# Stage two of a mixture-of-experts kernel: next rows' transposes, their copy and their quantisation at other places in the order

## The chip, the cores and the metric

The kernel runs on one core of a Trainium2 chip. The metric is device time in microseconds. Before the change three runs took 254.97, 255.40 and 255.97 us, median 255.4.

## What is computed

2048 rows of 512 numbers go through two expert layers. The first picks one of four experts by token id and uses one matrix three times, in f32 split into two halves. The second picks one of eight experts by the largest router logit, with weights cut to -1, 0, 1 and rows quantised to 8 bits ahead of each product:

```python
x = x + xattn(_layernorm(x), token_ids, ctx, ctx, ctx)      # silu(h W.T) * (h W.T), then W
x = x + ffn(_layernorm(x), router_w, wg, wu, wd)

def _weight_quant(w):
    s = 1.0 / jnp.clip(jnp.mean(jnp.abs(w)), EPS, None)
    return jnp.clip(jnp.round(w * s), -1.0, 1.0) / s
def _act_quant(x):
    s = 127.0 / jnp.clip(jnp.max(jnp.abs(x), axis=-1, keepdims=True), EPS, None)
    return jnp.clip(jnp.round(x * s), -128.0, 127.0) / s
# ffn, for every expert e, kept where the argmax of the logits is e
g = bitlinear(xf, wg[e])
u = bitlinear(xf, wu[e])
y = bitlinear(jnp.square(jax.nn.relu(g)) * u, wd[e])
```

## The kernel before, in words

Rows are sorted by expert into slots of 128, so that a slot has one expert. Stage one has 19 slots, stage two 23 (B2, numbered 0 to 22), which begin at about 172 us of the span. The weights of stage two are reduced to their signs during stage one and stay in SBUF as bf16. EARLY is 5: slots 0 to 4 are laid out before all rows are counted, slots 5 to 22 (late_rows) after.

One slot b of stage two takes this way, and a buffer name ending in 0 or 1 is that of the slot's parity:

- VectorE `quantise(b)` (L1304) makes the int8 rows t8 from the slot's rows, once they have landed (x1_in) and the transposes of slot b-2 have read the same buffer.
- TensorE `transpose_q(b)` (L1687, source t) turns them, in two transposes of pairs of int8, into PSUM bank 0. ScalarE `evict_tT(b)` (L783) copies that to qT.
- TensorE `gate_product(b)` and `up_product(b)` (L1695, source qT), each four matmuls 128x128 by 128x512. `load_ffn_expert` (L1707) loads the number of the next slot's expert into a register of TensorE's queue, by which the products pick their weights.
- ScalarE `relu_of(b)` (L791) and `square_of(b)` (L799); VectorE `product_of(b)` (L1314, prod), `largest_product` (L1324), `inverse_largest` (L1336) and `scale_from` (L1347); ScalarE `quantise_prod(b)` (L834) makes r8.
- TensorE `transpose_r(b)` (L1687, source r), ScalarE `evict_rT(b)` (L807), TensorE `down_product(b)` (L1695, source rT). VectorE `output(b)` (L1368) scales and adds; GpSimd computes the scale of the output (L642) and scatters the rows to memory (L652).

Each engine has its order written out by hand, in the five blocks of the program, and runs it strictly; semaphores join them. The slots overlap: at step u TensorE works on the gate and up products of slot u, the transposes of rows u+1, and transposes and down product of slots u-2 and u-3. ScalarE and VectorE have their own lists of steps u. SyncE loads the rows of each slot from memory (L411), in the order of the slots.

Of the kernel before, what the change touches and what calls it, by code (L numbers as in the profile page):

```python
# [24 lines left out]
B2 = TILES + E2 - 1  # L25
# [25 lines left out]
EARLY, EARLY_AFTER = 5, 14  # L51
# [42 lines left out]
def moe_program(nc, x_in, tokens_in, ctx_in, router_in, weights_in, out):  # L94
    with ExitStack() as whole:
# [161 lines left out]
        def cols_of(slots, col, n=1):  # L257

            if slots[0] < EARLY:
                tile, first = staged[slots[0] // 3], slots[0] % 3  # L260
            else:
                tile, first = late_rows, slots[0] - EARLY
            if len(slots) == 1:
                return tile[:, first * ROW + col:first * ROW + col + n]
            three = tile[:, first * ROW:(first + len(slots)) * ROW].rearrange("p (s c) -> p s c", c=ROW)
            return three[:, :, col:col + n]
# [16 lines left out]
        def pairs(transposed):  # L283
            return transposed.bitcast(I8)
# [397 lines left out]
        def _(act):  # L682
# [92 lines left out]
            def evict_tT(b):  # L775
                if not 0 <= b < B2:
                    return
                act.wait_ge(tT_ready, b + 1)
                if b >= 2:
                    act.wait_ge(u_ready, b - 1)  # L780
                else:
                    act.wait_ge(a_ready, B1)
                nc.scalar.activation(qT[b % 2][:, :], pairs(tT_ps), ACT.Copy).then_inc(qT_ready, 1)  # L783

            def relu_of(b):
                if not 0 <= b < B2:
                    return
                act.wait_ge(g_ready, b + 1)
                if b >= 1:
                    act.wait_ge(relu2_ready, b)  # L790
                nc.scalar.activation(relu[:, :], g_ps[b % 2][:, :], ACT.Relu).then_inc(relu_ready, 1)  # L791

            def square_of(b):
                if not 0 <= b < B2:
                    return
                act.wait_ge(relu_ready, b + 1)
                if b >= 1:
                    act.wait_ge(prod_ready, b)
                nc.scalar.activation(relu2[:, :], relu[:, :], ACT.Square).then_inc(relu2_ready, 1)  # L799

            def evict_rT(b):
                if not 0 <= b < B2:
                    return
                act.wait_ge(rT_ps_ready, b + 1)
                if b >= 2:
                    act.wait_ge(d_ready, b - 1)
                nc.scalar.activation(rT[b % 2][:, :], pairs(rT_ps), ACT.Copy).then_inc(rT_ready, 1)  # L807
# [16 lines left out]
            def copy_by_slot(late):  # L824
                act.wait_ge(blocks_ready, late + 1)
                nc.scalar.activation(by_slot[late][:, :], by_slot_ps[late], ACT.Copy).then_inc(by_slot_ready, 1)

            def quantise_prod(b):
                if not 0 <= b < B2:
                    return  # L830
                act.wait_ge(r_scale_ready, b + 1)
                if b >= 1:
                    act.wait_ge(rT_ps_ready, b)
                nc.scalar.activation(r8[:, :], prod[b % 2][:, :], ACT.Copy, scale=fac[b % 2][:, 2:3])\  # L834
                    .then_inc(r8_ready, 1)
# [47 lines left out]
            evict_tT(3)  # L883
            for u in range(2, B2 - 1):
                relu_of(u)
                if u in (3, 4, B2 - 2):


                    evict_tT(u + 1)
                square_of(u)  # L890
                if 4 < u < B2 - 2:
                    evict_tT(u + 1)
                if u == 4:
                    copy_by_slot(1)
                evict_rT(u - 2)
                quantise_prod(u - 1)
# [11 lines left out]
        def _(dve):  # L908
# [387 lines left out]
            def quantise(b):  # L1296
                if not 0 <= b < B2:
                    return
                dve.wait_ge(x1_in[b], 16)
                if b >= 2:  # L1300
                    dve.wait_ge(tT_ready, b - 1)
                else:
                    dve.wait_ge(hT_ready, B1)
                dve.tensor_scalar(t8[b % 2][:, :], cols_of([b], 0, D), cols_of([b], NEG), cols_of([b], SCALE),  # L1304
                                  ALU.add, ALU.mult).then_inc(t8_ready, 1)
# [207 lines left out]
            product_of(3)  # L1513
            for u in range(4, STEPS):
                largest_product(u - 1)
                if u > 4:
                    quantise(u + 1)
                if u in (B2 - 2, B2):
                    output(u - 4)
                inverse_largest(u - 1)  # L1520
                if u not in (B2 - 2, B2):
                    output(u - 4)
                scale_from(u - 1)
                product_of(u)

        @block.tensor
        def _(pe):
# [191 lines left out]
            def transpose_q(b):  # L1719
                if not 0 <= b < B2:  # L1720
                    return
                pe.wait_ge(t8_ready, b + 1)
                if b >= 1:
                    pe.wait_ge(qT_ready, b)
                    if b == EARLY + 1:

                        pe.wait_ge(by_slot_ready, 2)
                else:

                    pe.wait_ge(hT_lo_ready, B1)  # L1730
                transpose2(tT_ps, t8[b % 2]).then_inc(tT_ready, 1)

            def gate_product(b):
                if not 0 <= b < B2:
                    return
                pe.wait_ge(qT_ready, b + 1)
                if b >= 2:
                    pe.wait_ge(relu_ready, b - 1)
                if b == 0:

                    pe.wait_ge(cut_ready, MATS - 1)
                    pe.wait_ge(p_ready, B1)
                if b == 1:
                    pe.wait_ge(by_slot_ready, 1)
                product2(g_ps[b % 2], qT[b % 2], ffn_expert[b], 0).then_inc(g_ready, 1)

            def up_product(b):
                if not 0 <= b < B2:
                    return
                if b >= 2:  # L1750
                    pe.wait_ge(prod_ready, b - 1)
                if b == 0:
                    pe.wait_ge(pT_lo_ready, B1)
                if b == 1:
                    pe.wait_ge(x1T_copied, B1)
                product2(u_ps[b % 2], qT[b % 2], ffn_expert[b], 1).then_inc(u_ready, 1)
# [101 lines left out]
            transpose_r(0)  # L1858
            for u in range(3, B2 - 2):
                gate_product(u)  # L1860
                up_product(u)
                load_ffn_expert(u + 1)
                if u == 4:
                    spread_means(1)
                transpose_q(u + 1)
                transpose_r(u - 2)
                down_product(u - 3)

# [50 lines left out]
```

## Time and profile before

| what | value |
|---|---|
| median of three runs | 255.4 us |
| the profiled execution | 255.78 us |
| its span | 253.8 us |
| TensorE busy | 233.1 us, 92% |
| VectorE busy | 216.7 us, 85% |
| ScalarE busy | 210.9 us, 83% |
| GpSimd busy | 165.8 us, 65% |
| chain of waits, share of TensorE | 69% |
| granted TensorE clock | 0.996 |

The span goes from the first to the last instruction of the program; the execution takes about 2 us more. The busy time of TensorE (PE) is that of its matmuls, whose records overlap in a pipeline; PEld is its weight load. DVE is VectorE, ACT ScalarE, POOL GpSimd, SP SyncE. A small q behind an engine (PEldq, SPq) is its queue, the part that reads instructions and issues them. An engine that is not on the chain of waits may idle without cost. Times in the trace are microseconds from the start of the span.

### The profile page before, as it was taken

Reading aid. Unit: us, or ns where it says so; the run is one execution under the profiler, and the core shown is the slowest. Engines: PE = TensorE matmul, PEld = TensorE weight load, DVE = VectorE, ACT = ScalarE, POOL = GpSimd, SP = SyncE. Lnnn points to the kernel's source line nnn. Section 1 sums busy time; section 2 is a strip of 40 time slices with the busy share of each in tenths; the row PEclk is TensorE's granted clock in tenths of the full one; section 3 lists DMA queues with packets and bytes.
Section 4 is the critical chain, followed back from the end, with each engine's and each line's share of the span. In section 5 each row is a group of like instructions: output and inputs, shape, how many; then the busy total and the mean of one; then the engine's idle time right before and its main releaser. Section 6 shows DMA issues by size and latency. Waiting matters only on the chain.

```text
span 253.8 us, 5548 instructions
## 1 busy us (share of the span) xinstructions
PE 233.1 (92%) x1327; PEld 167.8 (66%) x1327; DVE 216.7 (85%) x675; ACT 210.9 (83%) x324; POOL 165.8 (65%) x325
## 2 busy tenths in 40 slices
PE   2398989999999999999999999999999999999980
PEld 2245778888888888888888888885344444444430
DVE  5889989799989988898888988879999888889871
ACT  2776899799888988898888888787898999999960
POOL 4363665868778777687777664347638786757653
PEclk9999999999999999999999999999999999999998
DMA  6999944946664499784576434651389952211110
GB/s 201 423 336 383 425 183 155 355 132 234 240 208 151 131 368 404 284 310 145 210 249 225 161 103 180 207 159 56 98 226 296 313 214 83 85 38 68 65 42 0
DMA packets 13725, 51.70 MB, mean 204 GB/s; under 512 B 2750, under 2 KB 2750, under 8 KB 10112
## 3 DMA queue, kind: packets, MB, share of 16 engines
q1 hardware_dynamic: 8816, 37.91, 42.8%
q0 software_dynamic: 4880, 13.44, 14.4%
q8 instruction: 13, 0.21, 0.4%
q14 instruction: 16, 0.13, 0.1%
HBM read 40.49 MB, written 13.48 MB: 213 GB/s over the span
## 4 chain that ended last, share of the span: by engine, by line
PE 69%; DVE 11%; DMA 11%; issue 5%; POOL 1%; ACT 1%; SPq 0%; DVEq 0%; ACTq 0%; POOLq 0%
PE bank L1573 33%; PE bank L1695 18%; PE bank L1557 8%; PE bank L1665 5%; DMA staged<-weight_chunks 5%; DMA ternary<-weight_chunks 3%; PE bank L1687 2%; DMA x<-x_rows,gather 2%; DVE ctx_lo L1009 1%; POOL out_rows L652 1%; DMA staged<-x_rows 1%; DVE ternary L966 1%; DVE t L1304 1%; DVE stats L1067 1%; PE bank L1592 1%
## 5 line engine op out<-in xcount | busy, mean ns | idle before, releaser
L1695 PE MATMUL bank<-ternary,qT 128*128 x184 | 44.2, 380 | 0.2
L703 ACT ACTIVATE ternary<-staged 128x2048 bf16<-128x2048 f32 x20 | 38.0, 1899 | 2.2 <-DMA staged<-weight_chunks 2.2
L709 ACT ACTIVATE ternary<-staged,w_scale 128x1536 int16<-128x1536 f32 x20 | 31.4, 1576 | 2.3 <-DVE w_scale L1023 0.6
L1695 PEld LDWEIGHTS bank<-ternary,qT 128*128 128x128 bf16 x184 | 17.8, 98 | 21.2 <-issue 6.2
L571 POOL DMA_INDIRECT x_rows<-row,store_at x19 | 25.3, 1330 | 6.8 <-POOL store_at L563 5.3
L482 POOL DMA_INDIRECT x<-x_rows,gather x16 | 18.5, 1155 | 10.4 <-DVE gather L978 6.3
L652 POOL DMA_INDIRECT out_rows<-late_rows,late_token x18 | 19.1, 1059 | 8.7 <-DVE late_rows L1368 6.4
L1695 PE MATMUL bank<-ternary,rT 128*128 x92 | 23.6, 380 | 0.3 <-ACT rT L821 0.3
L756 ACT ACTIVATE p<-bank,rstd 128x512 f32<-128x512 f32 x19 | 13.0, 685 | 12.0 <-PE bank L1573 12.0
L1573 PE MATMUL bank<-ctx_hi,pT_hi 128*128 x76 | 22.3, 415 | 0.1
L1103 DVE SCALAR_TENSOR_TENSOR p<-bank,rstd,p 128x512 f32<-128x512 f32 x19 | 14.2, 750 | 9.6 <-ACT p L756 9.6
L1573 PE MATMUL bank<-ctx_hi,hT_hi 128*128 x76 | 22.3, 414 | 0.0
L1665 PEld LDWEIGHTS bank<-router,x1T 128*128 128x128 f32 x152 | 19.7, 191 | 2.0 <-ACT x1T L765 0.6
L1573 PE MATMUL bank<-ctx_lo,hT_hi 128*128 x76 | 20.4, 390 | 0.2 <-DVE ctx_lo L1009 0.2
L1573 PE MATMUL bank<-ctx_lo,pT_hi 128*128 x76 | 20.6, 392 | 0.0
L1573 PE MATMUL bank<-ctx_hi,pT_lo 128*128 x76 | 20.5, 392 | 0.0
L526 POOL TENSOR_TENSOR row<-ln,half_powers 128x2 f32<-128x2 f32 x19 | 14.5, 763 | 9.1 <-DVE squares L1138 9.1
L1314 DVE TENSOR_TENSOR prod<-bank,relu 128x512 f32<-128x512 f32 x23 | 15.8, 689 | 5.4 <-issue 3.4
L1573 PE MATMUL bank<-ctx_hi,hT_lo 128*128 x76 | 20.3, 389 | 0.0
L1665 PE MATMUL bank<-router,x1T 128*128 128x8 f32 x152 | 18.2, 246 | 0.1
L498 POOL TENSOR_TENSOR rstd<-var_eps,half_powers 128x1 f32<-128x1 f32 x19 | 14.0, 734 | 4.8 <-DVE var_eps L1079 4.3
L834 ACT ACTIVATE r<-prod,fac 128x512 int8<-128x512 f32 x22 | 15.9, 721 | 0.9 <-DVE fac L1347 0.9
(237 smaller groups left out, 646.5 us busy)
## 6 DMA issues: line engine op xcount, KB each, us to landing
staged<-weight_chunks SPq DMA_DIRECT2D x20, 1024.0 KB, 5.3
late_rows<-x_rows SPq DMA_DIRECT2D x18, 260.0 KB, 3.2
ternary<-ctx_chunks SPq DMA_DIRECT2D x4, 1024.0 KB, 6.4
ternary<-weight_chunks SPq DMA_DIRECT2D x4, 1024.0 KB, 12.3
x_rows<-filler SPq DMA_DIRECT2D x1, 2080.0 KB
staged<-x_rows SPq DMA_DIRECT2D x5, 260.0 KB, 2.7
x_rows<-row,store_at POOLq DMA_INDIRECT x19, 6.0
out_rows<-late_rows,late_token POOLq DMA_INDIRECT x18
```

The lines of the kernel that those rows point to most:

```text
L482: pool.indirect_dma_start(x[b % RING], None, x_in, bass.IndirectOffsetOnAxis(ap=gather1[:, b:b + 1], axis=0), bounds_check=last_token, oob ...
L526: pool.tensor_tensor(r[:, RSTD:INV + 1], s[:, 2:4], half_powers[:, :], ALU.pow).then_inc(norm2, 1)
L571: pool.indirect_dma_start(x1_rows, bass.IndirectOffsetOnAxis(ap=store_at[b % ROWS][:, :], axis=0), row[b % ROWS][:, :], None, bounds_check ...
L652: pool.indirect_dma_start(out, bass.IndirectOffsetOnAxis(ap=token, axis=0), cols_of([b], 0, D), None, bounds_check=last_token, oob_is_err= ...
L703: nc.scalar.activation(ternary[:, m * K * D:(m + 1) * K * D], staged_of(i), ACT.Abs, accum_out=abs_sum[:, 2 * i:2 * i + 1]).then_inc(abs_r ...
L709: nc.scalar.activation(ternary[:, m * K * D + DVE_COLS:(m + 1) * K * D].bitcast(I16), staged_of(i)[:, DVE_COLS:], ACT.Copy, scale=w_scale[ ...
L834: nc.scalar.activation(r8[:, :], prod[b % 2][:, :], ACT.Copy, scale=fac[b % 2][:, 2:3])\
L1314: dve.tensor_tensor(prod[b % 2][:, :], u_ps[b % 2][:, :], relu2[:, :], ALU.mult)\
L1557: last = pe.transpose(ps[:, k * P:(k + 1) * P], src[:, k * P:(k + 1) * P], ident[:, :])
L1573: last = pe.matmul(ps[:, :], left[:, k * P:(k + 1) * P], right[:, bass.ds(e * (K * D) + k * D, D)], start=(n == 0 and k == 0), stop=(n == ...
L1665: last = pe.matmul(logits_ps[:, 0:E2], x1T[:, k * P:(k + 1) * P], router[:, k * E2:(k + 1) * E2], start=(k == 0), stop=(k == K - 1))
L1695: last = pe.matmul(ps[:, :], side(left[:, :], k), ternary[:, bass.ds(e * (3 * K * D) + (kind * K + k) * D, D)], start=(k == 0), stop=(k == ...
```

## The change

Three places of the hand-written order move, all of them in stage two, and no instruction is added or removed:

- On TensorE the transposes of the next rows stand between the gate and the up product, at steps 3 and 5 to 20. At step 4 they stay behind the up product.
- On ScalarE the copy of these transposes stands between relu and square at steps 3 to 21. Before it did so at steps 3, 4 and 21 only.
- On VectorE the rows are quantised two slots ahead, from step 4 on. Before it was one slot ahead.

```diff
@@ ScalarE
             for u in range(2, B2 - 1):
                 relu_of(u)
-                if u in (3, 4, B2 - 2):
+                if u > 2:
                     evict_tT(u + 1)
                 square_of(u)
-                if 4 < u < B2 - 2:
-                    evict_tT(u + 1)
                 if u == 4:
                     copy_by_slot(1)
                 evict_rT(u - 2)
@@ VectorE
             for u in range(4, STEPS):
                 largest_product(u - 1)
-                if u > 4:
-                    quantise(u + 1)
+                quantise(u + 2)
                 if u in (B2 - 2, B2):
                     output(u - 4)
@@ TensorE
             for u in range(3, B2 - 2):
                 gate_product(u)
+                if u != EARLY - 1:
+                    transpose_q(u + 1)
                 up_product(u)
                 load_ffn_expert(u + 1)
-                if u == 4:
+                if u == EARLY - 1:
                     spread_means(1)
-                transpose_q(u + 1)
+                    transpose_q(u + 1)
                 transpose_r(u - 2)
                 down_product(u - 3)
```

TensorE, a late step of an even slot, before. Bank 4 takes the gate product, bank 1 the up product, bank 0 the transposes of t8, bank 7 those of r8; ISA is a register instruction of the queue:

```order
L1695 MATMUL bank4<-ternary,qT0 128x512
L1695 ISA
L1695 MATMUL bank1<-ternary,qT0 128x512
...
L1695 MATMUL bank1<-ternary,qT0 128x512
L1707 TENSOR_LOAD expert2_1
L1707 ISA x2
L1687 MATMUL bank0<-ident16,t8_1 128x128 x2
L1687 MATMUL bank7<-ident16,r8 128x128 x2
```

And the same step after:

```order
L1690 MATMUL bank4<-ternary,qT0 128x512
L1682 MATMUL bank0<-ident16,t8_1 128x128 x2
L1690 ISA
L1690 MATMUL bank1<-ternary,qT0 128x512
...
L1690 MATMUL bank1<-ternary,qT0 128x512
L1702 TENSOR_LOAD expert2_1
L1702 ISA x2
L1682 MATMUL bank7<-ident16,r8 128x128 x2
L1690 ISA
L1690 MATMUL bank6<-ternary,rT1 128x512
```

The transposes of t8 have moved ahead of the up product; load and transposes of r8 stay behind it.

ScalarE, one step before (relu2 is the square, qT1 the copy of the next rows' transposes):

```order
L791 ACTIVATE relu<-bank4 128x512
L799 ACTIVATE relu2<-relu 128x512
L783 ACTIVATE qT1<-bank0 128x512
L807 ACTIVATE rT0<-bank7 128x512
L834 ACTIVATE r8<-prod1,fac1 128x512
```

and after:

```order
L791 ACTIVATE relu<-bank4 128x512
L783 ACTIVATE qT1<-bank0 128x512
L799 ACTIVATE relu2<-relu 128x512
L807 ACTIVATE rT0<-bank7 128x512
L834 ACTIVATE r8<-prod1,fac1 128x512
```

The copy has changed places with the square.

VectorE, from one product to the next, before (fac0 holds the largest product of the even slot and its scales):

```order
L1314 TENSOR_TENSOR prod0<-bank1,relu2 128x512
L1324 TENSOR_REDUCE fac0<-prod0 128x1
L1304 TENSOR_SCALAR t8_0<-late_rows 128x512
L1336 RECIPROCAL fac0<-fac0 128x1
L1368 SCALAR_TENSOR_TENSOR late_rows<-bank6,out_scale,late_rows 128x512
L1347 TENSOR_SCALAR fac0<-fac0,cap_scale 128x1
```

and after:

```order
L1310 TENSOR_TENSOR prod0<-bank1,relu2 128x512
L1320 TENSOR_REDUCE fac0<-prod0 128x1
L1300 TENSOR_SCALAR t8_1<-late_rows 128x512
L1332 RECIPROCAL fac0<-fac0 128x1
L1364 SCALAR_TENSOR_TENSOR late_rows<-bank6,out_scale,late_rows 128x512
L1343 TENSOR_SCALAR fac0<-fac0,cap_scale 128x1
```

The place in the row is the same; the buffer is the other one, since the slot is one further on.

## Rows read from the trace of the kernel before

**Rows 1.** Busy time by windows; columns: stretch, length, PE, PEld, DVE, ACT, POOL, clock, DMA

```profile
200.00:220.00 20.00, 19.85 (x105) 9.23 (x103) 17.62 (x39) 18.52 (x34) 15.08 (x30) 1.00 0.45 157
```

**Rows 2.** Page, groups of instructions; busy, mean ns, idle before

```profile
L1695 PE MATMUL bank<-ternary,qT 128*128 x184 | 44.2, 380 | 0.2
```

**Rows 3.** Timeline of one steady step; start, length, engine, instruction, idle before

```profile
197.10 0.69 DVE L1314 TENSOR_TENSOR prod<-bank,relu 128x512 f32<-128x512 f32 x1 [0.24 <-issue]
...
197.63 1.90 PE L1695 MATMUL bank<-ternary,qT 128*128 x8
...
198.43 0.54 DVE L1304 TENSOR_SCALAR t<-late_rows 128x512 int8<-128x512 f32 x1
...
198.70 0.60 ACT L791 ACTIVATE relu<-bank 128x512 f32<-128x512 f32 x1
...
199.33 0.63 ACT L799 ACTIVATE relu<-relu 128x512 f32<-128x512 f32 x1
...
199.37 0.28 PE L1687 MATMUL bank<-ident,t 128*128 128x128 bf16 x2
...
199.48 0.28 PE L1687 MATMUL bank<-ident,r 128*128 128x128 bf16 x2
...
199.60 0.21 DVE L1347 TENSOR_SCALAR fac<-fac,cap_scale 128x1 f32<-128x1 f32 x1
...
199.64 1.03 PE L1695 MATMUL bank<-ternary,rT 128*128 x4
...
199.87 0.58 ACT L783 ACTIVATE qT<-bank 128x512 bf16<-128x512 int8 x1
...
200.05 0.69 DVE L1314 TENSOR_TENSOR prod<-bank,relu 128x512 f32<-128x512 f32 x1 [0.24 <-issue]
...
200.59 1.90 PE L1695 MATMUL bank<-ternary,qT 128*128 x8
```

**Rows 4.** Instructions of line 1707; min/median/max ns, first and last start

```profile
L1707 PEldq TENSOR_LOAD <-expert x23: 301/308/632, 171.4 to 237.4; - x23
```

**Rows 5.** Timeline of PE: first, longest and last step from slot 6 to 21

```profile
191.73 1.89 PE L1695 MATMUL bank<-ternary,qT 128*128 x8
...
206.64 1.90 PE L1695 MATMUL bank<-ternary,qT 128*128 x8
...
208.65 0.27 PE L1687 MATMUL bank<-ident,t 128*128 128x128 bf16 x2
...
209.88 1.89 PE L1695 MATMUL bank<-ternary,qT 128*128 x8
...
237.03 1.03 PE L1695 MATMUL bank<-ternary,qT 128*128 x4
```

**Rows 6.** Timeline of PE, step 3: the transposes of slot 4

```profile
183.57 0.28 PE L1687 MATMUL bank<-ident,t 128*128 128x128 bf16 x2 [0.21 <-DVE t L1304]
```

**Rows 7.** Timeline of SP's queue and of DVE; page, DMA issues

```profile
182.90 5.79 SPq L411 DMA_DIRECT2D late_rows<-x_rows  x6
...
187.02 0.69 DVE L1324 TENSOR_REDUCE fac<-prod 128x1 f32<-128x512 f32 x1
...
late_rows<-x_rows SPq DMA_DIRECT2D x18, 260.0 KB, 3.2
```

**Rows 8.** Timeline of the tail, step 21 and on

```profile
238.10 0.60 ACT L791 ACTIVATE relu<-bank 128x512 f32<-128x512 f32 x1
...
238.74 0.60 ACT L783 ACTIVATE qT<-bank 128x512 bf16<-128x512 int8 x1
...
239.23 0.62 ACT L799 ACTIVATE relu<-relu 128x512 f32<-128x512 f32 x1
...
239.94 0.69 DVE L1314 TENSOR_TENSOR prod<-bank,relu 128x512 f32<-128x512 f32 x1 [0.53 <-ACT relu L799]
...
240.23 0.72 ACT L834 ACTIVATE r<-prod,fac 128x512 int8<-128x512 f32 x1
...
240.84 0.60 ACT L791 ACTIVATE relu<-bank 128x512 f32<-128x512 f32 x1
```

## The prediction, made before the changed kernel ran

> **What bounds the kernel now.** I read the page first: TensorE is busy all along, so the busy share decides nothing, and the change touches only stage two, the last 80 us. The table by windows then shows what stage two looks like [rows 1]: in 20 us TensorE is busy 19.85, but ScalarE 18.52 and VectorE 17.62, so three engines are nearly full and a shorter step of one needs room on the other two. The timeline of one step gives the rest.
>
> The price of a product comes from the page [rows 2]: a matmul record lasts 0.380 us, and eight in a row last 1.90 [rows 3], so they start (1.90 - 0.38) / 7 = 0.217 us apart. A step has twelve, 2.60. The two transposes of t8 begin 0.11 ahead of the two of r8 (199.37, 199.48), so four cost 0.22. TensorE's work in a step is 2.82 us. The step shown lasts 200.59 - 197.63 = 2.96. Its gap is at the gate product: the down product begins at 199.64 and is through its four starts at 200.51, while the copy into qT begins at 199.87, ends at 200.45, and the gate product starts 0.14 behind it, at 200.59. The copy can't come sooner: its transposes ran at 199.37, behind the up product. So each step goes round transposes, copy, gate product, with only one down product to cover the copy.
>
> Over the whole stretch, gate product 6 starts at 191.73 and gate product 21 at 237.03 [rows 5]: 45.30 us for 15 steps, 3.02 each, 0.20 above TensorE's work. The rest over 2.96 is in five longer steps of 3.08 to 3.24 (the longest, 206.64 to 209.88, is shown). There the t8 transposes start 208.65 - 206.64 = 2.01 after the gate product where 8 x 0.217 = 1.74 would do, 0.27 late. What stands between is the load of the next expert's number: 0.31 us as a median and 0.63 at most [rows 4]. TensorE's queue can issue nothing behind it meanwhile.
>
> **The change, part by part.**
>
> *Transposes between gate and up product (steps 3 and 5 to 20).* Same instructions. The copy now has up product, r8 transposes and down product to hide behind, 0.87 + 0.11 + 0.87 = 1.85 us, where it had 0.98. Taken from the gate product's start G: transposes at G + 0.87. The copy is behind relu on ScalarE; relu starts at G + 1.07 (198.70 - 197.63 [rows 3]); the copy follows 0.49 later, G + 1.56, ends at G + 2.15, and the next gate product may go at G + 2.29. TensorE needs until G + 2.82. The wait goes, with 0.5 to spare.
>
> *What is late next on TensorE* is the load of the expert's number. It stays behind the up product, in front of the r8 transposes. As the gate product no longer holds the queue, the queue comes to it earlier, so a short load is covered; the long ones (five of fifteen) cost between 0 and 0.27 each. I take 0.02 a step, near the lower end, because a product behind a held queue (206.64) shows the lateness and I remove the hold. Step: 2.84. The bounds for the step: 2.82, all covered, and 2.96, only the long ones gain nothing more than the row of a short step today.
>
> The Trainium skill, "TensorE: Matmul & The Clock Gate", Engine queue depths, gives TensorE a queue of 64 instructions. By it the loads would be wholly hidden and a step 2.82, the lower bound above. This trace can't confirm the depth, as the gate product is waited for in the steps shown; the sum does without it.
>
> *The copy between relu and square.* ScalarE in this order can be read in the tail, where before has it already [rows 8]: copy to square 0.49, square to r8 1.00 (with the rT copy in it), r8 to relu 0.61. With 0.49 from relu to copy (where the copy needn't wait) that is 2.59 a step, below 2.84. The square starts at relu + 0.98 instead of + 0.63, so the product on VectorE comes 0.35 later: before, square 199.33, ends 199.96, product 200.05, i.e. relu + 1.35; after, relu + 1.70 or G + 2.77. VectorE between two products, without the wait: from the product at 197.10 to the end of the scale at 199.81, 2.71 us [rows 3], again below 2.84, so it keeps up though it runs later against TensorE. Its next link: the scale of product u-1 ends 2.71 after that product, at G - 2.84 + 2.77 + 2.71 = G + 2.64; r8 is wanted at relu + 1.98 = G + 3.05. That leaves 0.4. The round that joins the two engines, r8, relu, copy, square, product (0.61 + 0.49 + 0.49 + 0.72) and on through maximum and scale to the r8 after next (2.71 + 0.1), is 5.12 us for two steps, 2.56 a step. All three engines fit into 2.84.
>
> *Rows quantised two slots ahead.* With the transposes in front of the up product, t8 is wanted 0.87 sooner. Left one slot ahead it would be too late: it starts 1.33 after the product of the step before (198.43 - 197.10 [rows 3]), at G - 2.84 + 2.77 + 1.33 = G + 1.26, ends at G + 1.80, and its transposes are due at G + 0.87. Two ahead, it is done 1.9 before it is wanted. The count of instructions is the same except that t8 of row 6 comes at step 4 instead of 5. Its row must have landed: issues start at 182.90, six in 5.79 us, so row 6 is issued by 184.0 and lands 3.2 later, 187.2 [rows 7]; VectorE reaches it 0.6 after the maximum at 187.02, at 187.6. Hidden, by 0.4. If not, VectorE stands some tenths once.
>
> *Steps 3 to 5.* Here the change costs. The transposes of step 3 wait for t8 of row 4 until 183.57 in both kernels [rows 6]; before, both products of step 3 were ahead of that wait and lay in it, so that TensorE idled only 0.21 by the row. After, the up product is behind it: 183.57 + 0.14 + 0.87 = 184.58. And the load, issued from a queue that was just held, is bare. From the long step: eight issues and a load of 0.63 took 2.01 [rows 4, 5]. Four issues fewer save at most half of the 1.38 beside the load, which leaves 1.32, or 1.00 with a load of 0.31, and there is 0.87 of work to cover it: 0.13 to 0.45 bare, taken as 0.3. Then r8 transposes and down product, 0.98 and the start of a held product 0.14: gate product 4 at 186.0. Step 4 keeps its order, 2.96: 188.96. Step 5 at 2.82: its wait for t8 of row 6 is gone. Gate product 6: 191.78, against 191.73. The loss and the gain of the first steps cancel, 0 +- 0.5.
>
> *Steps 6 to 20*: 15 x (3.02 - 2.84) = 2.7 us saved.
>
> *Tail.* Product 21 starts at 239.94, 2.91 behind gate product 21 [rows 5, 8]; relu is on time (238.10), but the copy waits 0.15 for transposes that wait for t8. After, G + 2.77: 0.15 saved. From there VectorE's chain is as before, ending in the scatters.
>
> Sum: -0.05 + 2.7 + 0.15 = 2.8. The profiled execution took 255.78 (span 253.8): 253.0. The median of the runs shown, 255.4, is 0.38 below it: **252.6 us**.
>
> **The rivals.**
>
> *A. Long loads stay bare.* All five long steps keep 0.2 to 0.27, and step 3 is at its bad end: 1.2 us less gain, 253.8. For it: the load is at the same place against the next transposes [rows 5]. Against: the queue is no longer held at each gate product.
>
> *B. The bound is another engine, nothing is gained.* ScalarE is busy 18.52 of 20 us, VectorE 17.62 [rows 1]. If those waits that look like slack are latency that reappears (product waits for square, r8 for scale), a step stays near 3.0 and time is 255.4 less 0 to 1, about 255. Against: both sums of starts are 2.59 and 2.71. The Trainium skill, "Perfetto Trace Analysis", Identifying the Most-Contended Engine, says to judge TensorE by weight-load busy share and not by matmul busy share. Weight loads are 9.23 of 20 us here, so by that rule ScalarE is the engine to relieve and this is the case that follows; the gap in front of the gate product in the steady step speaks against it, but not against a small remainder.
>
> *C. Slower.* The place is ScalarE's queue, in front of the square. The copy is now ahead of the square, so whatever makes the transposes late (a long load, t8, a bare queue) delays square, product, maximum, scale and r8, all in one line. It decides when the copy is held beyond relu + 0.49 by more than the free part of the two-step round, 2 x 3.02 - 5.1 = 0.9 us, in most steps. If it takes a step to 3.12, 15 x 0.10 = 1.5, with the 1.0 of step 3 not won back at step 5: 255.4 + 2.5 = 257.9. Against: the transposes stand at G + 0.87, 0.4 before their copy's turn, and t8 has a whole step.
>
> **How the numbers follow.** Forecast (252.0 to 253.3) 0.60; A 0.16; B 0.15; C 0.09. A measurement here can tell 0.5% from no change, that is 254.1 to 256.7. Forecast and A are faster, B nearly all same, C slower: 0.76, 0.15, 0.09. The range starts at 251.8 (step 2.82, loads of step 3 covered: 0.3 + 0.3 + a little) and goes to 254.6, the bound of a 2.96 step, which takes in A and the near part of B.
>
> **What would show it.** Gate products 6 to 21 in the trace after: 2.82 to 2.86 apart, the transposes right behind the fourth matmul. No idle between down and gate product. Product behind relu by 1.70. Gate product 4 near 186.0, an idle time at step 3 ahead of the transposes of about 1 us; gate product 6 near 191.8. Wrong if steps stay at 2.95 or more, if r8 waits for its scale, if t8 of row 6 waits for its row, or if waits of 0.2 and more stand in front of the r8 transposes.

## The result, and the profile after

| | before | after |
| --- | --- | --- |
| median of the runs, us | 255.87 (254.97 to 256.35, 6 runs) | 253.19 (252.79 to 253.79, 6 runs) |
| ratio, 95% interval | | 0.990 [0.9878, 0.9922] |
| profiled execution: time, span, us | 255.78, 253.8 | 253.38, 251.4 |
| mean granted clock | 0.996 | 0.994 |

The kernel is faster by 2.7 us, or 1.0%. The forecast was 252.6 in a range of 251.8 to 254.6, from a median of 255.4 for the kernel before; with six runs that median is 255.87, so that 0.47 of the 0.59 between 252.6 and 253.19 lies in the starting point. In the changed kernel the line of the products is 1690, of the transposes 1682, of the load of the expert's number 1702, of the product on VectorE 1310, of its maximum 1320, of t8 1300 and of the scale 1343; ScalarE's lines are the same.

The first answer to read is the table by windows, over the same 20 us as [rows 1], with the same columns:

```profile
200.00:220.00 20.00, 19.89 (x115) 10.10 (x116) 19.06 (x45) 19.20 (x36) 15.68 (x31) 1.00 0.48 170
```

All engines do more in the same 20 us: TensorE 115 matmuls for 105, VectorE 19.06 us for 17.62, ScalarE 19.20 for 18.52. TensorE's busy time hardly moved (19.85 to 19.89), since waits of 0.1 to 0.3 us between matmuls don't show in it.

A steady step of the changed kernel, from the timeline, answers to [rows 3]:

```profile
198.30 1.03 PE L1690 MATMUL bank<-ternary,qT 128*128 x4
...
199.17 0.27 PE L1682 MATMUL bank<-ident,t 128*128 128x128 bf16 x2
...
199.28 1.03 PE L1690 MATMUL bank<-ternary,qT 128*128 x4
199.37 0.60 ACT L791 ACTIVATE relu<-bank 128x512 f32<-128x512 f32 x1
...
199.86 0.59 ACT L783 ACTIVATE qT<-bank 128x512 bf16<-128x512 int8 x1
...
200.14 0.27 PE L1682 MATMUL bank<-ident,r 128*128 128x128 bf16 x2
...
200.75 0.21 DVE L1343 TENSOR_SCALAR fac<-fac,cap_scale 128x1 f32<-128x1 f32 x1
...
201.06 0.69 DVE L1310 TENSOR_TENSOR prod<-bank,relu 128x512 f32<-128x512 f32 x1
...
201.14 1.03 PE L1690 MATMUL bank<-ternary,qT 128*128 x4
201.34 0.73 ACT L834 ACTIVATE r<-prod,fac 128x512 int8<-128x512 f32 x1
```

The copy ends at 199.86 + 0.59 = 200.45, and the gate product follows at 201.14, 0.69 later: it no longer waits for the copy. The step is 201.14 - 198.30 = 2.84. The product stands 201.06 - 199.37 = 1.69 behind relu, and r8 begins 0.38 after the scale's end at 200.96.

Over the stretch of [rows 5], with the steps ahead of it, on the timeline of TensorE:

```profile
184.24 0.28 PE L1682 MATMUL bank<-ident,t 128*128 128x128 bf16 x2 [1.08 <-DVE t L1300]
...
186.61 1.89 PE L1690 MATMUL bank<-ternary,qT 128*128 x8
...
189.58 1.03 PE L1690 MATMUL bank<-ternary,qT 128*128 x4
...
191.55 0.13 PEld L1682 LDWEIGHTS bank<-ident,r 128*128 128x128 bf16 x2 [0.46 <-ACT r L834]
191.58 0.27 PE L1682 MATMUL bank<-ident,r 128*128 128x128 bf16 x2
...
192.68 1.03 PE L1690 MATMUL bank<-ternary,qT 128*128 x4
...
234.90 1.03 PE L1690 MATMUL bank<-ternary,qT 128*128 x4
```

From gate product 6 (192.68) to gate product 21 (234.90) it is 42.22 us, 2.815 a step, where it was 45.30 and 3.02. The first rows are the price. The transposes of step 3 wait 1.08 for t8, not 0.21 [rows 6], and gate product 4 starts 2.37 behind them; before it was 1.38, as the experiment that undoes this place shows again below.

The load of the step shown above, in the form of [rows 4] (over all 23 loads the times are 299, 308 and 674 ns):

```profile
L1702 PEldq TENSOR_LOAD <-expert x1: 674/674/674, 198.9 to 198.9; - x1
```

It is the longest one of this execution. It begins 0.6 behind the gate product's start, and the r8 transposes still come at 200.14, right behind the up product: it costs 0.02 at most (the step is 2.84). Before, one of 632 ns made the long step of 3.24. Not every long load is hidden, though: in a second profile of the same changed kernel (the run beside the experiment on step 3, below) one took 897 ns,

```profile
L1702 PEldq TENSOR_LOAD <-expert x1: 897/897/897, 198.3 to 198.3; - x1
```

and there the r8 transposes came 0.10 late (at 199.65, due at 199.55), the down product another 0.11 late, and the step was 200.75 - 197.70 = 3.05.

And the tail, product 21:

```profile
237.65 0.69 DVE L1310 TENSOR_TENSOR prod<-bank,relu 128x512 f32<-128x512 f32 x1 [0.35 <-ACT relu L799]
```

It is 237.65 - 234.90 = 2.75 behind gate product 21, where it was 239.94 - 237.03 = 2.91. Product 22 wins another 0.11 (2.45 behind product 21, it was 2.56).

The account of the two profiled executions, in us: transposes of step 3 to gate product 6, +0.28 (8.44 for 8.16); 15 steps, -3.08; tail, -0.16 - 0.11. That is -3.07. What lies ahead of it, which the change doesn't touch, put the transposes of step 3 at 184.24 and not 183.57, +0.67. Of this 0.55 is there already at relu of slot 0 (176.23 for 175.68), and it is a difference between executions: in the second profile of the changed kernel that relu starts at 175.66. Together -2.40, the difference of the spans. The medians, with more runs, say -2.7.

### The profile page after: what moved, and what is told of

Its sections match the earlier page's. It is cut to its first block, busy times and chain, and to the rows that moved or that the text cites. A ratio compares the mean times of both kernels' runs of the same rounds, so it can differ in the third digit from the quotient of the medians.

```text
span 251.4 us, 5540 instructions
## 1 busy us (share of the span) xinstructions
PE 229.9 (91%) x1319; PEld 167.5 (67%) x1327; DVE 216.9 (86%) x675; ACT 208.8 (83%) x324; POOL 166.2 (66%) x325
## 4 chain that ended last, share of the span: by engine, by line
PE 72%; DVE 10%; DMA 9%; issue 4%; POOL 1%; ACT 1%; SPq 0%; DVEq 0%; ACTq 0%; POOLq 0%
PE bank L1568 34%; PE bank L1690 20%; PE bank L1552 9%; PE bank L1660 5%; DMA staged<-weight_chunks 5%; DMA ternary<-weight_chunks 3%; PE bank L1682 2%; PE bank L1794 2%; POOL out_rows L652 1%; DMA staged<-x_rows 1%; DVE ternary L962 1%; DVE ctx_lo L1005 1%; PE bank L1587 1%; DMA token_ids<-token_ids_in 1%; DVE ternary L1024 1%
## 5 line engine op out<-in xcount | busy, mean ns | idle before, releaser
L1690 PE MATMUL bank<-ternary,qT 128*128 x179 | 45.4, 379 | 0.7 <-ACT relu L791 0.3
L1690 PEld LDWEIGHTS bank<-ternary,qT 128*128 128x128 bf16 x184 | 17.2, 98 | 16.4 <-issue 1.8
```

The costliest lines, as they stand in the source:

```text
L1690: last = pe.matmul(ps[:, :], side(left[:, :], k), ternary[:, bass.ds(e * (3 * K * D) + (kind * K + k) * D, D)], start=(k == 0), stop=(k == ...
```

## The experiments

My theory: the gate product waits for the copy from PSUM, and with the wait gone TensorE's own work (2.82 us a step) is the bound. It left two things open: which of the three edits takes the wait away, and whether loads of the expert's number cost anything because they are long, or because the queue of TensorE comes to them late. Ratios are against runs of the kernel before on the same chip (medians 255.88, 255.79 and 255.82 for the three groups). A difference can be told from 0.5% on, 1.3 us; below that I lean on the traces. Where a time is divided by 15, it runs from relu of slot 6 to relu of slot 21 in that run's profile (45.31 before, 42.22 after). A load is called bare where TensorE has no work to cover it.

### One part at a time

VectorE's edit alone: in the kernel before, only

```diff
-                if u > 4:
-                    quantise(u + 1)
+                quantise(u + 2)
```

> Of the three edits only the one on VectorE: rows quantised two slots ahead. My theory (the steady step is paced by transposes, copy, gate product): steps 6 to 20 stay at 2.95 to 3.02 us, since t8 was in time there; only the wait for t8 of row 6 at step 5 (0.7) and that at step 21 (about 0.4) go. 0.5 to 1.1 us faster than before, about 255.0 where before is 255.9. Rival (t8 is what the steps wait for, as the tags of the weight loads say): steps fall to 2.82, 3 us faster.

Measured: 255.69, ratio 0.999 [0.9970, 1.0009]. No change that can be told from noise. The wait for t8 at step 5 did go, but gate product 6 then waited for its copy:

```profile
191.65 1.90 PE L1694 MATMUL bank<-ternary,qT 128*128 x7 [0.47 <-ACT qT L783]
```

It starts 191.65 - 188.05 = 3.60 behind gate product 5, where it was 191.73 - 187.92 = 3.81. The new t8 at step 4 stands in front of the scale of product 3 on VectorE, so r8 and behind it relu 5, square and copy came later on ScalarE (r8 1.11 behind gate product 5, before 0.82). So 0.2 us of the expected 0.7 is there. Steps 6 to 20 were 45.70 / 15 = 3.05 long; in this run more loads were long, up to 841 ns. The expectation was too high for the first reason, and what VectorE alone gives is within what the loads vary from run to run.

TensorE and VectorE changed, ScalarE as before (copy behind the square):

```diff
-                if u > 2:
+                if u in (3, 4, B2 - 2):
                     evict_tT(u + 1)
                 square_of(u)
+                if 4 < u < B2 - 2:
+                    evict_tT(u + 1)
```

> TensorE and VectorE as changed, ScalarE as before (copy behind the square at steps 5 to 20). My theory: the copy ends at relu + 1.16 + 0.6 = G + 2.83 and the gate product can start 0.14 later, at G + 2.95 to 2.97, so the wait in front of the gate product stays although the transposes are early. Steps 2.95, the long ones of before gone; the loss of 1 us at step 3 stays: 0.3 faster to 0.5 slower than before. Rival (the place of the transposes is what counts): steps 2.82, as fast as the whole change, 2.7 us faster.

Measured: 256.75, ratio 1.0037 [1.0017, 1.0057]. A step on the timeline:

```profile
207.68 1.04 PE L1694 MATMUL bank<-ternary,qT 128*128 x4
...
208.56 0.28 PE L1686 MATMUL bank<-ident,t 128*128 128x128 bf16 x2
...
208.76 0.60 ACT L791 ACTIVATE relu<-bank 128x512 f32<-128x512 f32 x1
...
209.39 0.63 ACT L799 ACTIVATE relu<-relu 128x512 f32<-128x512 f32 x1
...
209.92 0.58 ACT L783 ACTIVATE qT<-bank 128x512 bf16<-128x512 int8 x1
...
210.64 0.60 PE L1694 MATMUL bank<-ternary,qT 128*128 x2
```

The transposes are there at 208.56, and the copy begins only at 209.92, 1.16 behind relu, because the square is in front of it. The gate product follows the copy's end (210.50) by 0.14, and the step is 2.96, to the hundredth what it was before [rows 3]. So the copy's place on ScalarE alone held the gate product: relu 1.08 behind the gate product, copy 1.16 later, 0.58 for it and 0.14 to start. The early transposes without the copy's new place gain nothing and pay the loss of step 3.

ScalarE and VectorE changed, TensorE as before (transposes behind the up product):

```diff
                 gate_product(u)
-                if u != EARLY - 1:
-                    transpose_q(u + 1)
                 up_product(u)
                 load_ffn_expert(u + 1)
-                if u == EARLY - 1:
+                if u == 4:
                     spread_means(1)
-                    transpose_q(u + 1)
+                transpose_q(u + 1)
```

> ScalarE and VectorE as changed, TensorE as before (transposes of t8 behind the up product). My theory: the copy can run 0.31 after transposes at G + 1.74, so at G + 2.05 to 2.64, and the gate product may start at G + 2.78, just ahead of the 2.82 that TensorE needs: steps 2.82 to 2.88, without the loss at step 3. 2.5 to 3.5 us faster than before, at least level with the whole change; the move on TensorE would then be worth nothing by itself. Rival (the move on TensorE is what brings the gain; without it loads of the expert's number push transposes, copy, square and product all later): steps 2.95 or more, under 1 us faster.

Measured: 252.99, ratio 0.9889 [0.9869, 0.9909]: level with the whole change. The same step:

```profile
208.40 1.89 PE L1690 MATMUL bank<-ternary,qT 128*128 x8
...
210.12 0.28 PE L1682 MATMUL bank<-ident,t 128*128 128x128 bf16 x2
...
210.44 0.60 ACT L783 ACTIVATE qT<-bank 128x512 bf16<-128x512 int8 x1 [0.16 <-PE bank L1682]
...
211.22 1.03 PE L1690 MATMUL bank<-ternary,qT 128*128 x4
```

Here the copy waits 0.16 for transposes behind the up product, and yet the step is 211.22 - 208.40 = 2.82: the copy begins 0.32 behind its transposes, not 0.50 as in [rows 3], and that is enough. Over steps 6 to 20 the copy stands 0.71 to 0.99 behind relu, where 0.49 would do, and the steps take 43.06 / 15 = 2.87. The whole change has 2.815, so the move on TensorE brings about 0.8 us over these steps, and loses 1.0 at step 3.

Without VectorE's edit, the other two in place:

```diff
-                quantise(u + 2)
+                if u > 4:
+                    quantise(u + 1)
```

> TensorE and ScalarE as changed, VectorE as before (rows quantised one slot ahead). My theory: a ring closes, transposes, copy (+0.31), square (+0.49), product (+0.72), maximum, t8 (+1.33 and 0.54), transposes (+0.1): 3.47 us a step in place of 3.02. 16 steps: 6 to 8 us slower than before. Rival (t8 has slack enough): as fast as the whole change.

Measured: 266.13, ratio 1.0395 [1.0352, 1.0438], more than expected. A step:

```profile
208.54 0.69 DVE L1310 TENSOR_TENSOR prod<-bank,relu 128x512 f32<-128x512 f32 x1 [0.87 <-PE bank L1691]
...
209.26 1.03 PE L1691 MATMUL bank<-ternary,qT 128*128 x4
...
209.87 0.54 DVE L1300 TENSOR_SCALAR t<-late_rows 128x512 int8<-128x512 f32 x1
...
210.46 0.29 PE L1683 MATMUL bank<-ident,t 128*128 128x128 bf16 x2 [0.17 <-DVE t L1300]
210.58 1.03 PE L1691 MATMUL bank<-ternary,qT 128*128 x4
...
211.29 0.63 ACT L799 ACTIVATE relu<-relu 128x512 f32<-128x512 f32 x1
...
211.85 0.27 PE L1683 MATMUL bank<-ident,r 128*128 128x128 bf16 x2 [0.24 <-issue]
212.01 0.69 DVE L1310 TENSOR_TENSOR prod<-bank,relu 128x512 f32<-128x512 f32 x1 [0.77 <-PE bank L1691]
...
212.95 1.03 PE L1691 MATMUL bank<-ternary,qT 128*128 x4
```

t8 ends at 210.41 and its transposes go at 210.46, 1.20 behind the gate product, where 0.87 is due. The up product behind them comes late, and the r8 transposes, due at 210.58 + 0.87 = 211.45, come at 211.85, another 0.40 late with the load in front of them. So the next gate product starts only at 212.95, with it relu, square and product come late, and so does the t8 after them: the lateness feeds itself. The round takes two steps: product to the transposes of t8 210.46 - 208.54 = 1.92, from there to the next gate product 2.49, gate product to product 212.01 - 209.26 = 2.75, together 7.16, or 3.58 a step. Measured is 3.57 (53.61 / 15).

That is a ring, but not the one that I had expected. The row puts the product's wait down to the up product; yet the product stands 0.72 behind the square, as in the kernels before and after, and the last record of the up product ended at 211.61, 0.40 ahead of it. And the copy was not held: it stands 0.50 behind relu (once in these steps ScalarE waited 0.2 us for the transposes). The ring closes through TensorE's own order, up product, r8 transposes, down product, gate product; the copy in front of the square only adds its usual 0.35 to it. VectorE's edit earns nothing itself and is what makes the early transposes possible.

### Step 3

The whole change, with the transposes of step 3 back behind the up product:

```diff
-                if u != EARLY - 1:
+                if u >= EARLY:
                     transpose_q(u + 1)
                 up_product(u)
                 load_ffn_expert(u + 1)
-                if u == EARLY - 1:
-                    spread_means(1)
+                if u < EARLY:
+                    if u == EARLY - 1:
+                        spread_means(1)
                     transpose_q(u + 1)
```

> The whole change, but on TensorE the transposes of step 3 stay behind the up product as before; the new place holds from step 5 on. My theory: gate product 4 comes 1.4 us behind the transposes of step 3 and not 2.4, ScalarE passes 0.65 of that on to steps 5 and 6, the steps stay at 2.82. 0.6 to 1.0 us faster than the whole change, about 252.4 where that has 253.2. Rival (the late t8 of row 4 and the chain on VectorE set steps 4 to 6 anyway): level with the whole change.

Measured: 252.21, ratio 0.9862 [0.9839, 0.9884]. The whole change ran beside it, unchanged:

> The whole change once more, on the same chip as the others of this call, for comparison: 253.2 where before has 255.9, by every theory.

It took 252.98, ratio 0.9893 [0.9872, 0.9914], 0.77 more. The intervals overlap a little; the traces decide. TensorE's timeline:

```profile
184.21 0.29 PE L1682 MATMUL bank<-ident,t 128*128 128x128 bf16 x2 [0.20 <-DVE t L1300]
...
185.58 1.24 PE L1690 MATMUL bank<-ternary,qT 128*128 x5
...
188.56 1.03 PE L1690 MATMUL bank<-ternary,qT 128*128 x4
...
191.65 0.59 PE L1690 MATMUL bank<-ternary,qT 128*128 x2
```

Gate product 4 stands 1.37 behind the transposes and not 2.37; everything later is alike, 2.98 and 3.09 for the next two steps and 2.81 from there. This order is the best of the study with all weights right, 3.6 us faster than the kernel before.

One more try on it, for the 3.09 of step 5: at step 4 VectorE does the scale ahead of the output.

```diff
-                if u not in (B2 - 2, B2):
+                if u not in (4, B2 - 2, B2):
                     output(u - 4)
                 scale_from(u - 1)
+                if u == 4:
+                    output(u - 4)
```

> The version with step 3 in the old order on TensorE, and at step 4 on VectorE the scale of product 3 ahead of the output of slot 0. Its trace shows gate product 6 coming 3.09 behind gate product 5, because r8 of slot 3 waits for that scale. My theory: 2.82 instead of 3.09 there, so 0.2 to 0.3 us faster than the version without this edit, about 252.0 where before has 255.8. Rival (VectorE is the later one there, product 4 comes 0.2 later and takes it back): no change.

Measured: 252.17, ratio 0.9861 [0.9827, 0.9894]: no difference. Gate products 5 and 6 are still 190.80 - 187.71 = 3.09 apart. The edit did what it should on ScalarE: r8 begins 0.81 behind gate product 5 and not 1.11. The transposes of r8 stayed where they were, 1.99 behind it. The theory had taken the wait that the profile puts down to r8 at its word, in the version without this edit, where r8 ends only 0.16 ahead of its transposes. The row at 191.55 of the changed kernel, "0.46 <-ACT r", could have warned: r8 there began at 190.39 and took 0.73, so it was done at 191.12, 0.43 ahead. Something else came last.

### The load

The whole change without the loads: the expert's number is read for slots 0 and 5 only and kept for the others.

```diff
-                ffn_expert[b] = pe.value_load(...)
+                    ffn_expert[b] = pe.value_load(...)   # slots 0 and 5 only
+                else:
+                    ffn_expert[b] = ffn_expert[b - 1]
```

> The whole change with the expert's number loaded only for slots 0 and 5, as in the run of before without loads (most slots multiplied with another expert's weights, the work the same in size). My theory: steps 6 to 20 are at TensorE's 2.82 already, so nothing is to be had there; only step 3, where the load stands bare, and the first steps of stage two gain: 0.2 to 0.8 us faster than the whole change. Rival (loads still cost something each step): 2 us faster.

Measured: 251.94, ratio 0.9851 [0.9807, 0.9895], 1.2 less than the whole change (1.0 less than the run of it above), a little more than expected; the intervals of the two just overlap. TensorE's timeline, with r8 of step 5:

```profile
183.83 0.28 PE L1682 MATMUL bank<-ident,t 128*128 128x128 bf16 x2 [1.49 <-DVE t L1300]
...
185.79 1.89 PE L1690 MATMUL bank<-ternary,qT 128*128 x8
...
188.77 1.03 PE L1690 MATMUL bank<-ternary,qT 128*128 x4
...
189.58 0.73 ACT L834 ACTIVATE r<-prod,fac 128x512 int8<-128x512 f32 x1
...
190.60 0.28 PE L1682 MATMUL bank<-ident,r 128*128 128x128 bf16 x2
...
191.58 0.59 PE L1690 MATMUL bank<-ternary,qT 128*128 x2
```

r8 of step 5 stands 0.81 behind the gate product in both kernels, but the transposes now follow at + 1.83 and not + 2.00, and gate product 6 at 2.81 and not 3.10. So that wait was for the queue and not for r8: the load there took an ordinary 0.31. At step 3 gate product 4 comes at 1.96 for 2.37. Of these 0.41, 0.28 lie ahead of the r8 transposes (0.99 behind those of t8 for 1.27) and 0.11 behind them. These are the two places where the queue has just been held (by t8, and by the copy at step 5). The fifteen steps after are 42.08 / 15 = 2.805 long against 2.815: there it is 0.01 a step. One caution: with one expert number throughout, most register instructions in front of the matmuls are gone too, so all these differences are those of loads and register instructions together.

The same in the kernel before:

> The kernel before, with the expert's number loaded into TensorE's register only for slots 0 and 5 and kept for the slots behind them, so that most slots are multiplied with another expert's weights; the work is the same in size. My theory: the five longer steps of before (3.08 to 3.24) come from this load standing in front of the transposes; without it all are 2.95, 45.3 us for 15 steps become 44.3: 0.8 to 1.2 us faster than before. Rival (the longer steps have another cause, for instance GpSimd's work at that time): no faster than 0.3.

Measured: 253.68, ratio 0.9913 [0.9883, 0.9944], 2.1 less. More than expected. Its step:

```profile
197.56 1.90 PE L1695 MATMUL bank<-ternary,qT 128*128 x8
...
199.80 0.58 ACT L783 ACTIVATE qT<-bank 128x512 bf16<-128x512 int8 x1
...
200.43 0.82 PE L1695 MATMUL bank<-ternary,qT 128*128 x3
```

Nearly all steps are 2.87 or 2.88 (43.15 / 15). The long ones were made by loads: in the kernel before, the five steps of 3.08 to 3.24 are the very ones whose loads took 505 to 632 ns, while the other ten had loads of 0.30 to 0.31. But the short ones shrank too, 2.96 to 2.87: the gate product starts 200.43 - 200.38 = 0.05 behind the copy and not 0.14. With one expert number throughout, the register instruction in front of each matmul is gone as well (24 of them are left of 276), so the queue has less to do at the moment it is let go. This is an edit of two things at once, and the split (15 x 0.09 = 1.3 for the start, 0.8 for the loads) is worked out from the rows, not measured apart.

Each load twice, in the whole change:

```diff
                 ffn_expert[b] = pe.value_load(...)
+                pe.value_load(...)
```

> The whole change with every load of an expert's number made twice. My theory: TensorE's queue needs about 2.7 us a step to issue what a step holds, and a load with its register instructions 0.6, so that two loads make it 3.3 and the queue becomes the bound: 0.4 to 0.5 more a step, 7 to 9 us slower than the whole change. Rival (loads are hidden by a queue that runs far ahead): less than 1 us slower.

Measured: 268.09, ratio 1.0479 [1.0435, 1.0523], 15 us slower, twice what I expected of it. The steps are 52.62 / 15 = 3.51:

```profile
208.53 1.03 PE L1690 MATMUL bank<-ternary,qT 128*128 x4
...
209.50 1.03 PE L1690 MATMUL bank<-ternary,qT 128*128 x4
...
210.74 0.27 PE L1682 MATMUL bank<-ident,r 128*128 128x128 bf16 x2 [0.21 <-issue]
...
211.85 0.38 PE L1690 MATMUL bank<-ternary,qT 128*128 x1
```

The r8 transposes are due at 210.37 and come at 210.74 for the queue ("issue"), step after step. One load is hidden by the queue's lead, and that lead is small: a second one uses it up, and the queue, not the engine, sets the step. Where both loads of a step take the usual 0.30 or 0.31, the step is 3.30 to 3.48, the 0.5 and a little more that I had expected; the long loads, now with nothing to cover them, do the rest (one of 0.85 makes a step of 3.86). Of the 15 us, 10.4 are in these fifteen steps and some 5 in the steps ahead of slot 6, which I had left out. The two loads of a step start 0.6 to 0.7 apart, so a load with the register instructions behind it takes the queue about 0.65; taken from the shortest steps of 3.30 this leaves, as an estimate, 2.65 to 2.7 us of the queue's time in a step of 2.82 with one load. So the queue gains only 0.1 to 0.2 on the engine in each step.

The load in the kernel before, moved behind the transposes:

```diff
                 up_product(u)
-                load_ffn_expert(u + 1)
                 ...
                 transpose_q(u + 1)
                 transpose_r(u - 2)
+                load_ffn_expert(u + 1)
                 down_product(u - 3)
```

> The kernel before with one edit: the load of the next expert's number stands behind the two pairs of transposes, in front of the down product, at steps 3 to 20; all weights are the right ones. My theory after the run without loads (2.1 us faster, steps of 2.87): of the 0.20 a step above TensorE's 2.82, 0.06 to 0.07 is long loads that hold back the t8 transposes, and the rest is the wait for the copy and the queue's register step behind it, which stays. Steps 2.95 to 3.00, 0.3 to 1.0 us faster than before. Rival (what the run without loads gained was the loads alone, short ones too): steps 2.87, 2 us faster. Second rival (a load costs what it costs wherever it stands): no change.

Measured: 259.71, ratio 1.0155 [1.0117, 1.0194], slower by 3.9; I had expected it faster, and no rival had this sign. The steps are 47.57 / 15 = 3.17 on average, from 2.96 to 3.97. One of 3.23:

```profile
210.70 0.28 PE L1687 MATMUL bank<-ident,r 128*128 128x128 bf16 x2
...
211.22 1.03 PE L1695 MATMUL bank<-ternary,rT 128*128 x4 [0.24 <-issue]
```

The load of this step begins at 210.4 and takes 0.31. The down product is 0.52 behind the r8 transposes, where 0.11 would do. Behind the transposes the load also stands behind the queue's waits for t8 and r8 (t8 ended at 210.18), so it starts when TensorE has nearly caught up, 1.5 behind the gate product. Where it was, it began 0.9 behind the gate product and ran beside the up product's matmuls.

## Why the prediction was right, and where not

**The step, 3.02 to 2.84.** Right: 2.815, just under the floor of 2.82 that I had worked out. Fifteen steps gave 3.08 for the 2.7 forecast. Of the 0.02 a step that I had put in for loads about 0.01 was spent (2.815 for 2.805 in the run without loads; 2.83 in the second profile, with its load of 897 ns).

**Why the copy was late.** This step of my argument was wrong: "The copy can't come sooner: its transposes ran at 199.37". The rows that I quoted say otherwise: the copy began 0.50 behind them, with the square running until 199.96 in between. The run with ScalarE's old order keeps 2.96 with early transposes; the one with TensorE's old order reaches 2.82 with late ones. The price of the bundle came out because both moves were in it, but the 2.7 us are there without TensorE's edit, which wins 0.8 in the steps and loses 1.0 at step 3: it is the moved line on ScalarE together with VectorE's, which alone gives nothing. ScalarE's move by itself wasn't tried, so whether it needs VectorE's stays open.

**Steps 3 to 5, -0.05 and up to 0.5 either way.** Gate product 4 at 2.37 behind the transposes (2.43 forecast), gate product 5 after 2.97 (2.96). At step 3 the load was bare by 0.28, as I had taken it (0.3). Step 5 was 3.10 for 2.82: the term that was mis-sized. I took the load to be bare at step 3 only, but gate product 5 is still held by its copy, which ends at 189.40 for a start at 189.58, and with the t8 transposes now in front of the up product the queue has more to issue ahead of the load than in a step of the kernel before, where a held gate product and a short load went together without loss. Net 0.28 lost where 0.05 was forecast.

**Tail.** -0.16 on product 21 as forecast (0.15), and 0.11 on product 22 that I had not counted.

**ScalarE and VectorE keep up.** Right. Product at relu + 1.69 (1.70 forecast), at gate + 2.76 (2.77); r8 had 0.38 to spare (0.4). t8 of row 6 stood right behind the maximum of step 4 and waited for no row.

**The rivals.** A (long loads stay bare) did not happen in the profiled execution: its loads of 674, 632 and 414 ns were hidden, and what was bare at steps 3 and 5 (0.7 us in all) were ordinary loads of 0.31 behind a held queue. The load of 897 ns in the second profile was bare by 0.2. B (another engine) didn't happen. The Trainium skill, "Perfetto Trace Analysis", Identifying the Most-Contended Engine, would still point to ScalarE: weight loads are 10.10 of 20 us and ScalarE is busy 19.20. The section sets the share of peak arithmetic (MFU) beside the weight loads, and the prediction left that out. An estimate with the 78.6 TFLOP/s of the same page: twelve matmuls of 128x128 by 128x512 in 2.96 us are 87% of peak, in 2.815 us 91%, without the transposes. That shows TensorE far nearer its limit than the weight loads do, though still below ScalarE's 96%. But the step is at the length of TensorE's own work, so in this kernel the measured spacing of its matmuls decides and not that share. C (the copy held on ScalarE delays everything behind it) decided in no run. The kernel without VectorE's edit is 10 us slower, but by the ring through TensorE, with its copy on time. The copy was held in the run with TensorE's old order, by 0.2 to 0.5 and so less than the 0.9 that C asks for, and its steps were 2.87.

**The depth of the queue.** By the Trainium skill, "TensorE: Matmul & The Clock Gate", Engine queue depths, the queue holds 64, and from that I had concluded that the loads would be hidden. With one load a step they nearly are, at 2.815; with two they aren't, at 3.51. Room for 64 gives no lead as long as the queue's own instructions take nearly as long as the engine's work (an estimated 2.7 of 2.82). What counted here was the time per instruction; no run here shows the depth.

**Luck** had a part in how close the number came: in the profiled execution the time up to step 3 was 0.67 longer, which differs between executions of the same kernel, and the first steps lost 0.23 more than forecast, while the steps gained 0.4 and the tail 0.1 more.

## What to carry to other kernels

When a product waits for a copy, look at what stood in front of the copy on its own engine before moving the copy's inputs: the gap between an input's end and the copy's start (0.50 here, where 0.32 is enough) tells which order to change. An edit that only gives room (t8 two slots ahead) is worth nothing by itself, and the bundle without it is 13 us slower, so test bundles by leaving out one part, not only by adding one. And put a register load of TensorE's queue where the queue is ahead, in the shadow of matmuls already issued and never behind a wait; apply such a reordering from the step on at which the pipeline is full, and leave the first steps as they were.

## What the runs showed of the hardware

- The load of a number into a register of TensorE's queue took 0.30 us at the least and 0.30 or 0.31 as a median in every profile with 23 of them, but the longest one took from 0.59 us (the version with step 3 in the old order) to 1.05 us (the load moved in the kernel before). Which ones were long changed from run to run. I found no cause; it stays open.
- A gate product held for its copy started 0.14 us behind the copy's end in the kernel before, and 0.05 in the same kernel with neither the loads nor most of the register instructions in front of its matmuls.
- One extra load a step costs 0.5 us a step or a little more where all loads are short (3.30 to 3.48 for 2.815) and 0.70 on average, more than the 0.31 of its record: register instructions of 0.15 and 0.02 us follow it, and behind it the next long load has nothing to cover it.
- A releaser named in a row can be one that was long done: 0.43 us ahead in the case of r8, 0.40 in that of the up product. The run with the scale first and the run without loads showed what did not and what did come last for r8.
